# Loads of the third tile's stack issued behind the transfer of the second tile's first maxima

## The reference

```python
def _layernorm(x, eps=1e-05): ...
def xattn(q, k, v, gamma):                    # (16, 64, 256) -> heads of (8, 256)
    qk = einsum('bhdq,bhdl->bhql', qh, kh) / sqrt(8)
    sm = softmax(qk, axis=-1)
    return gamma * einsum('bhql,bhdl->bhdq', sm, vh).reshape(B, Dv, Lq)
def ffn(x, w_gate, w_up, w_down, ln_weight):
    h = silu(bit_linear(x, w_gate)) * bit_linear(x, w_up)      # 8-bit rows, ternary weights
    h = rms_norm(h, ln_weight)
    return bit_linear(h, w_down)
x = x + xattn(_layernorm(x), ctx_2048, ctx_2048, gamma)
x = x + ffn(_layernorm(x), w_gate, w_up, w_down, ln_weight)
```

## Time and profile before

| what | value |
|---|---|
| median of three runs | 205.41 us (201.14, 205.41, 215.77) |
| profiled execution | 201.32 us, span 199.5 us |
| mean granted TensorE clock | 0.966 |
| PE, DVE, ACT, POOL busy | 88%, 77%, 69%, 56% of the span |
| chain that ended last | PE 44%, POOL 21%, DVE 13%, ACT 9%, issue 8%, DMA 4% |
| longest single piece of that chain | DMA `q_stack<-mt`, 7.66 us, from 35.40 us on |
| VectorE's wait for `x_sb` | 4.3 us, once |

### The profile page before, as it was taken

How to read it: one execution, slowest core, us unless ns; L and a number is a source line. 1 busy time by engine, 2 the same in 40 slices (tenths; PEclk the granted TensorE clock), 3 DMA queues, 4 the chain that set the end, 5 groups by cost and what they waited for, 6 DMA issues and landing times.

```text
span 199.5 us, 4665 instructions
## 1 busy us (share of the span) xinstructions
PE 174.6 (88%) x1563; PEld 102.9 (52%) x1572; DVE 154.4 (77%) x301; ACT 138.2 (69%) x277; POOL 111.1 (56%) x279
## 2 busy tenths in 40 slices
PE   7999999958849987888899899999989988998783
PEld 5557566535525444544565465566446634634342
DVE  6696468627697597889998998999899895456783
ACT  2353477527947697888887897889689877772562
POOL 6962363506777678889753842755284266324260
PEclk9999999987996799999999999999999997999999
DMA  5957978880137347112273720017100000000001
GB/s 155 195 168 173 238 217 287 185 199 2 43 98 169 93 123 155 43 55 54 63 190 105 192 47 32 0 40 181 52 0 6 31 3 4 5 26 0 0 0 56
DMA packets 14413, 18.38 MB, mean 92 GB/s; under 512 B 2357, under 2 KB 12997, under 8 KB 13381
## 3 DMA queue, kind: packets, MB, share of 16 engines
q1 hardware_dynamic: 13414, 16.69, 33.0%
q10 hardware_dynamic: 975, 1.39, 2.8%
HBM read 14.03 MB, written 3.80 MB: 89 GB/s over the span
## 4 chain that ended last, share of the span: by engine, by line
PE 44%; POOL 21%; DVE 13%; ACT 9%; issue 8%; DMA 4%; POOLq 0%; ACTq 0%; DVEq 0%
PE psO L701 9%; PE psA L645 6%; PE psB L681 5%; POOL hw L448 4%; PE psA L630 4%; DMA q_stack<-mt 4%; PE psG L795 3%; DVE h L1168 2%; DVE gu L1157 2%; ACT th L943 2%; ACT probs L861 2%; POOL hrms L1304 2%; PE psB L660 2%; DVE mneg L1049 2%; PE psG L610 2%
## 5 line engine op out<-in xcount | busy, mean ns | idle before, releaser
L1049 DVE TENSOR_REDUCE mneg<-psA 128x2 f32<-128x512 f32 x124 | 79.6, 679 | 10.0 <-PE psA L645 6.6
L861 ACT ACTIVATE probs<-psB 128x512 f32<-128x512 f32 x119 | 68.2, 597 | 10.0 <-PE psB L681 5.7
L681 PE MATMUL psB<-q_stack,k_stack 75*128 75x256 bf16 x216 | 42.0, 278 | 7.2 <-ACT probs L861 4.0
L645 PE MATMUL psA<-k_stack,q_stack 72*128 72x256 bf16 x224 | 43.0, 277 | 2.2 <-DVE mneg L1049 2.2
L701 PE MATMUL psO<-probs,vt 128*32 128x256 f32 x480 | 34.7, 410 | 0.2 <-ACT probs L861 0.2
L448 POOL TENSOR_TENSOR hw<-h,lnw 128x512 f32<-128x512 f32 x13 | 16.5, 1274 | 25.1 <-DVE h L1168 20.1
L681 PEld LDWEIGHTS psB<-q_stack,k_stack 75*128 75x128 bf16 x216 | 18.3, 99 | 18.8 <-ACT probs L861 7.9
L645 PEld LDWEIGHTS psA<-k_stack,q_stack 72*128 72x128 bf16 x224 | 18.3, 98 | 16.7 <-issue 8.6
L701 PEld LDWEIGHTS psO<-probs,vt 128*32 128x32 f32 x480 | 13.1, 114 | 12.9 <-issue 6.9
L943 ACT ACTIVATE th<-psG,tscale 128x512 f32<-128x512 f32 x14 | 9.6, 687 | 9.0 <-PE psG L795 8.8
L1157 DVE SCALAR_TENSOR_TENSOR gu<-th,psG 128x512 f32<-128x512 f32 x14 | 9.6, 687 | 7.8 <-ACT th L943 7.8
(11 more groups left out here) (187 smaller groups left out, 335.1 us busy)
## 6 DMA issues: line engine op xcount, KB each, us to landing
k_stack<-k_scratch SPq DMA_DIRECT2D x21, 192.0 KB
q_stack<-q_scratch SPq DMA_DIRECT2D x18, 192.0 KB
q_scratch<-q_parts SPq DMA_DIRECT2D x21, 64.0 KB, 2.9
k_scratch<-k_parts SPq DMA_DIRECT2D x18, 64.0 KB, 2.7
w_sb<-in_L_ffn_w_gate_dram SPq DMA_DIRECT2D x1, 1024.0 KB, 8.7
w_sb<-in_L_ffn_w_up_dram SPq DMA_DIRECT2D x1, 1024.0 KB, 10.1
w_sb<-in_L_ffn_w_down_dram SPq DMA_DIRECT2D x1, 1024.0 KB, 5.5
out_dram<-y_sb SPq DMA_DIRECT2D x8, 128.0 KB, 1.8
```

Source lines behind the costliest of these rows:

```text
L645: mm = pe.matmul(a_home(k)[:, qt * L:(qt + 1) * L], q_stack[0:STACK, t % NBUF, bh, qt * P:(qt + 1) * P], k_stack[0:STACK, t % NBUF, bh, :] ...
L681: mm = pe.matmul(b_home(b)[:, lt * L:(lt + 1) * L], k_stack[:, t % NBUF, bh, lt * P:(lt + 1) * P], q_stack[:, t % NBUF, bh, :], start=True ...
L861: act.activation(probs[:, b_unit(b) % RING, :], bank[:, :], ACT.Exp, scale=SCALE).then_inc(s_exp, 1)
L1049: dve.tensor_reduce(mneg[:, k % MBUF, QT * (bh % HALF):QT * (bh % HALF + 1)], bank[:, :].rearrange("p (q l) -> p q l", q=QT), AX.X, ALU.ma ...
```

## The change

The step at which SP issues the six loads of tile 2's stack goes from 52 to 53. At step 52 SP now meets only the transfer of the maxima k = 2, and waits there for ScalarE's copy to `mt`; the six loads come behind it, and then, at step 54, the inputs of tiles 4 to 7 as before. No instruction is added or removed, and no wait.

```diff
-LOAD_AT = (19, 52, 70, 89, 135, 153, 197)
+LOAD_AT = (19, 53, 70, 89, 135, 153, 197)
```

## The result

The changed kernel took 206.8 us in the median of four runs (203.98, 204.32, 209.35, 219.02) beside 203.3 us for the kernel before; the ratio is 1.0153, 95% interval 1.011 to 1.0197. A second comparison on one chip, eleven runs of before and six of the change, gave 1.0453, 1.0364 to 1.0541, with medians of 202.4 and 212.4 us. So the change makes the kernel slower; by how much, 1.5% or 4.5%, the two comparisons do not agree, and the first alone lies within the 2% that the prediction calls no change. Both kernels scatter with the time that TensorE is granted only the half clock, and the ratios leave the disturbed runs out.

What follows compares the result with a forecast made beforehand. Two nearly equal paths bound the stretch, TensorE's through the maxima and VectorE's through x: x 4.35 us later less 0.5 slack gives +3.85, clock +0.45, so 201.3 + 4.3 = 205.6, given as 206.0 us, range 202.5 to 211.0.

Steps and rivals of the forecast that it cites:

- the 2% that the prediction calls no change: Whole kernel: about 2%, 4 us, is what a measurement can tell from no change; within 2% had chance 0.44.
- The time and its sign: Whole kernel: 206.0 us, a slowdown of 2.1% in the profiled execution; chance of slower 0.54.
- Two nearly equal paths, 0.5 us of slack: Before tile 2: TensorE's path waits 2.41 us for maxima; VectorE's path through x has only 0.5 us of slack.
- When things land: SP's queue: maxima land at 37.9, tile 2's stack at about 45.5, x at 49.9, later by 4.35 us.
- the upper bound: Landing of x: all shifted like the first stack load, by 4.66 us, so x lands at 50.2.
- The path behind x: From x through statistics, `rstd`, split and transpose to ScalarE's `mt` copy: +3.85 us there, TensorE standing for a bank until about 51.
- The stack's wait "alone would cost nothing": A of unit 32: TensorE waits from about 42.7 to 45.5, losing most of the saving; alone no cost against before.
- The clock term: TensorE's half clock after its stands, over about 51 to 55 us: +0.45 us, bounds nothing to 2 us.
- Rival 3: Half clock lasts through the first feed forward groups: 2 to 5 us on top, 207.5 to 211; chance 0.14.
- Rival 1: Fast transfers take up the shift, x lands before 46.1: 200.5 us, not slower; chance 0.08.
- Rival 2: A later wait, as at 53.09, shrinks and gives back 1 to 2.5 us: 202.5 to 204.5; chance 0.10.

Runs made afterwards that it cites:

- (2): Kernel before, with the maxima k = 2 issued by ScalarE on its own queue, SP's loads and inputs unchanged; second comparison 1.0104 (0.999 to 1.0218).
- (3): Kernel before, with SP waiting for the copy to `mt` ahead of the six loads, maxima still behind them; ratio 1.0187 (0.9847 to 1.0527).
- the second profile: Changed kernel run once more beside the kernel before, nothing else changed; profiled execution 220.3 us, ratio 1.0453 (1.0364 to 1.0541).
- (7): Changed kernel plus idle matrix products where TensorE stands, 20 ahead of A of unit 33, 10 ahead of the maxima's transpose; 205.0, 209.4, 219.7, 222.9 us.
- (5): Changed kernel with inputs early, stack late: inputs ahead of the stack (203.7 to 221.1 us, two sets), or inputs on ScalarE's queue (ratio 1.0211).
- (6): Kernel before with inputs, stack, maxima in SP's queue (203.0 to 204.9 us), or inputs, stack, `w_down` with maxima on ScalarE's queue (ratio 1.028).

## Why the prediction was right, and where not

**The time and its sign.** 206.0 forecast, 206.8 measured (212.4 in the second comparison, over the upper end of 211). The forecast slowdown of 2.1% lies between the two ratios. In part this is luck: the cost was forecast as 4.3 us, and the ratios stand for 3.1 us in the first comparison and 9.0 in the second.

**Two nearly equal paths, 0.5 us of slack.** Borne out by the traces: the chain of the first profile of before runs through the maxima, that of the second through x, and the copy moved 2.66 us where x moved 3.1. That early maxima alone gain only the slack is not shown: in (2) they were not early, and in (3) the late ones held the copy up by up to 0.95 us.

**When things land.** Issues as computed. Counted from the issue of the maxima, the stack was forecast at 10.1 us and seen at 10.05 in the second profile (10.8 in the first, where nobody waited for it); x was forecast at 14.5 and came at 13.5 and 14.0. That term was 0.5 to 1.0 us too large: the last three microseconds moved 290 GB/s at a share of 0.99, faster than the 260 GB/s of the last three before. The Trainium skill, page DMA: Bandwidth & Descriptors, section on why a DMA increments its semaphore by 16, would have put x still later, by which the sum was worse. Its count of engines agrees with the trace, where the six loads raise the stack's semaphore in 78 steps, 13 to a load (by that section 12 engines and one addition of the issuing sequencer), and each input raises its own in 16; what failed is that x therefore lands near the upper bound.

**The path behind x.** Right where the clock was full: A of unit 33 was forecast at 15.6 us behind the issue of the maxima and seen at 15.3 in the second profile; the copy k = 3 was forecast at 19.0 and came at 18.0, 18.6 and, in (7), 18.75. VectorE's wait of 8 to 9 us is the 8.30 of (7), and there TensorE waited 3.2 us for the stack, where 2.8 was forecast. The profile of the result itself shows neither: its waits are 3.8 us and none, and B of unit 16 came at 44.35 and not at 40.8, because TensorE was at the half clock from 35 us on, which the prediction did not foresee.

**The stack's wait "alone would cost nothing".** Neither shown nor refuted. The stack landed when forecast and x later still, so it never bounded the changed kernel, and the runs of (5), with x moved out of its way, did not keep its landing: it came 2 to 3 us later and cost as much, 17.85 and 18.10 us of stretch. What the change delays is one block of 2.2 MB, and its last part lands 12.6 to 14.1 us after the issue of the maxima in each of the three orders. Blaming x was right for the changed kernel and wrong as a cure.

**The clock term.** The place was right, about 52.8 to 63 us where I had said 51 to 55, and the size too small: 0.45 us taken; from copy k = 3 to k = 4 the change was 1.0 us over before, which had its own half clock at 61 to 67.7 us, and 1.8 to 2.2 over the profile of (7). (The clock of before came back at 47.2 us, not at 47.8.) At copy k = 3, where +3.85 was forecast, the change was late by 2.66 us. That it was late by 3.75 at the last copy and by 2.7 at the end comes near the forecast by chance: gains and losses of 2.3 and 2.4 us lie between, and 1 us came back at 167 us, where before stood at the half clock. Rival 3, by which the clock costs more (207.5 to 211), describes the second comparison, where three of the six times of the change are 207.2 to 207.7.

**Rival 1** (x not late) fell with the landing at 48.65. **Rival 2** (taken up later) is not refuted. In the first profile what came back was half clock of the kernel before; but in (3) the span kept only 0.3 of the 2.5 us lost in the stretch, and no run tells how much of that is a later wait grown shorter and how much is chance.

## What to carry to other kernels

A wait of a DMA in the chain is worth only its lead over the next path, here 0.5 us in the first profile, so look for the engine that stands at the same time for another transfer. Moving a short transfer ahead of long ones is free only if it is ready; here the long ones waited 4.5 us for a copy on another engine, with empty queues, and everything behind them in the queue came late. And a stand of the matrix engine may be paid twice, since the clock can fall behind it. Last, look at the landing before calling a transfer early: a queue of its own did not make it early in (2) and (6).

## What the runs showed of the hardware

- Two DMAs of 512 KB landed 3.7 and 5.1 us after their issue on ScalarE's queue, just ahead of the six loads in SP's queue, and 3.9 and 4.8 us after it on SP's own queue ahead of these loads; behind them they took 7.6 and 8.4. The last of the six loads then took 8.88 us; in the second profile of the changed kernel it was at most 5.9 us (issued at 54.6, used at 60.48).
- The 12 KB of the maxima took 2.3 us ahead of the loads (issued at 35.19, last update of the semaphore at 37.51), 7.66 us behind them in SP's queue, and 6.80 and 9.5 us on ScalarE's queue, issued after loads and inputs or weights on SP's. So in these runs the order of issue counted for more than the queue. The Trainium skill, page DMA: Bandwidth & Descriptors, section on queues, rings and completion order, says that an engine takes turns between the queues that it has work for; these times do not show it, and no run tests it by itself.
- The kernel before had spans from 195.8 to 218.3 us on one chip within one comparison, with mean clocks of 0.974 and 0.859: 10 and 62 us at the half clock. That is five times the 4.3 us that were forecast. The time between two fixed instructions of a profile, with its clock beside it, told more of the mechanism than the times did, but it does not add up to the span.
